# The end of layer 0: fills in runs of eight rows, the last chunk placed in two halves, counts one step earlier

## The reference

```python
x = x + ffn0(cond0(x))            # silu(x W1) * (x W3), Hadamard transform, W2
h = x W^T + scaled adapter(x)     # layer 1, condition: one of 8 adapters of rank 16 per batch
logits = h gate                   # 32 experts
w, idx = top_k(softmax(logits), 4); w = w / w.sum()
x = x + sum over the 4 chosen experts e of w_e * down_e(up_e(h) * silu(gate_e(h)))
```

## Time and profile before

| | |
|---|---|
| runs of the kernel | 1116.61 us median of 3, 1112.86 to 1117.81 |
| the profiled execution | 1120.59 us, of which its span is 1118.8 us |
| PE busy / weight loads | 898.6 us (80%) / 693.5 us |
| DVE, ACT, POOL busy | 565.7, 357.8 and 354.0 us |
| mean granted clock of PE | 0.894 |
| layer 0's last product ends / first block load is issued | about 214.8 us / 272.2 us |

### The profile page before, as it was taken

How to read it: one execution, slowest core, us unless ns; L and a number is a source line. 1 busy time by engine, 2 the same in 40 slices (tenths; PEclk the granted TensorE clock), 3 DMA queues, 4 the chain that set the end, 5 groups by cost and what they waited for, 6 DMA issues and landing times.

```text
span 1118.8 us, 17568 instructions
## 1 busy us (share of the span) xinstructions
PE 898.6 (80%) x5301; PEld 693.5 (62%) x5301; DVE 565.7 (51%) x1656; ACT 357.8 (32%) x996; POOL 354.0 (32%) x387
## 2 busy tenths in 40 slices
PE   2999898701999999698338768897996898999976
PEld 2778676501777777574236656787644676777765
DVE  5646775420565655158427666855252434444322
ACT  3434242320333333011126655750252222221210
POOL 7100616271455555113433434200046102333000
PEclk9999898965999999898658988996996998999997
DMA  9051206465544443482257778600052202332131
GB/s 346 12 188 38 77 4 241 154 223 169 182 128 132 126 131 87 156 276 79 77 118 172 167 157 174 157 36 1 27 167 86 86 5 67 107 99 72 53 104 46
DMA packets 71900, 132.25 MB, mean 118 GB/s; under 512 B 19652, under 2 KB 54237, under 8 KB 69347
## 3 DMA queue, kind: packets, MB, share of 16 engines
q1 hardware_dynamic: 49027, 75.81, 22.4%
q0 software_dynamic: 20480, 53.19, 17.7%
q10 hardware_dynamic: 2304, 2.13, 0.6%
HBM read 87.39 MB, written 43.30 MB: 117 GB/s over the span
## 4 chain that ended last, share of the span: by engine, by line
PE 29%; DMA 10%; issue 5%; DVE 3%; ACT 2%; SPq 1%; another core or an unknown queue 1%; POOL 1%; DVEq 0%; POOLq 0%; ACTq 0%
PE ps L442 8%; PE ps L680 4%; PE ps L698 3%; DMA early<-early 3%; DMA early<-newblk,new_i 2%; PE ps L2295 2%; DMA big<-early 2%; PE ps L2147 1%; PE ps L2189 1%; PE ps L2250 1%; DMA big<-newblk,new_i 1%; DMA early<-big 1%; SPq L920 1%; PE ps L2116 1%; DMA early<-in_cache,win_i 1%
## 5 line engine op out<-in xcount | busy, mean ns | idle before, releaser
L764 POOL DMA_INDIRECT sent_d<-mid,slot_i x88 | 94.8, 1078 | 134.3 <-DVE mid L598 88.7
L755 POOL DMA_INDIRECT back_d<-early,mid x95 | 93.8, 987 | 103.7 <-DVE early L739 70.5
L698 PE MATMUL ps<-early 96*128 (+1 forms) x346 | 100.0, 389 | 0.3 <-DVE early L733 0.2
L726 DVE TENSOR_TENSOR early<-early,ps 128x96 f32<-128x96 f32 (+1 forms) x134 | 37.3, 278 | 116.6 <-ACT early L714 77.9
L680 PE MATMUL ps<-big,early 128*128 x380 | 89.5, 360 | 5.9 <-ACT early L709 3.4
L709 ACT ACTIVATE early<-ps 128x256 f32<-128x256 f32 x134 | 51.3, 383 | 133.4 <-PE ps L670 122.9
L476 DVE TENSOR_TENSOR hidl<-work,hidh 128x512 fp32r<-128x512 f32 (+1 forms) x56 | 38.7, 691 | 102.6 <-ACT hidh L469 97.0
L670 PE MATMUL ps<-late,mid 128*128 128x128 f32 x268 | 53.6, 283 | 34.8 <-DMA mid<-sent_d 34.8
L482 ACT ACTIVATE work<-ps 128x512 f32<-128x512 f32 (+1 forms) x56 | 33.3, 595 | 149.2 <-PE ps L442 134.9
L755 POOL DMA_INDIRECT back_d<-big,mid x39 | 38.4, 984 | 118.5 <-DVE big L739 114.3
L680 PEld LDWEIGHTS ps<-big,early 128*128 128x128 f32 x380 | 62.6, 198 | 19.3 <-issue 16.4
(11 more groups left out here) (384 smaller groups left out, 2105.5 us busy)
## 6 DMA issues: line engine op xcount, KB each, us to landing
mid<-sent_d SPq DMA_DIRECT2D x134, 130.0 KB
big<-back_d SPq DMA_DIRECT2D x16, 512.0 KB
early<-back_d SPq DMA_DIRECT2D x16, 256.0 KB, 3.3
sent_d<-big SPq DMA_DIRECT2D x26, 130.0 KB
early<-in_w SPq DMA_DIRECT2D x3, 1024.0 KB, 11.7
big<-in_gate SPq DMA_DIRECT2D x1, 3072.0 KB, 12.2
big<-in_up SPq DMA_DIRECT2D x1, 3072.0 KB, 19.5
early<-in_gu SPq DMA_DIRECT2D x1, 2816.0 KB, 10.9
```

The costliest lines, as they stand in the source:

```text
L698: last = nc.tensor.matmul(ps[:, 6 + j % 2, 0:D], L.hTb[j % 2][0:f1 - f0, h * P:(h + 1) * P], L.down[0:f1 - f0, h, bass.ds(owners[j] * D, D ...
L726: nc.vector.tensor_tensor(L.hb[j % 2], L.sgb[j % 2], ps[:, 2 + j % 2, F:2 * F], ALU.mult)\
L755: nc.gpsimd.indirect_dma_start(out=back_d, out_offset=bass.IndirectOffsetOnAxis(ap=xblk[b % XRING][:, D:D + 1].bitcast(I32), axis=0), in_= ...
L764: nc.gpsimd.indirect_dma_start(out=sent_d, out_offset=bass.IndirectOffsetOnAxis(ap=L.slot_i[:, i:i + 1], axis=0), in_=L.rows[c][:, t, n, : ...
```

## The change

- Fills of layer 1: a fill still writes the same 128 rows of `sent_d`, but from 16 partitions that hold eight rows each (`FILL` = 8, `fill_rows`), so as 16 pieces of 8,320 B. `filler` is now 2,080 words of `work` on each partition, written by DVE in two memsets and a third for the mark, where GpSimd wrote it before. The partitions rotate with the expert's number. Layer 3 keeps its fills (`filler3`).
- The last chunk is two pieces of two tiles (`pieces`). Each is chosen, counted, numbered and weighted by itself; GpSimd's first half of scatters needs only the first. `dve_ends` and the table follow the second half's share products.
- In the steps: `pe_count` moves from m=6 to m=5, `act_share` in front of step 6's silu, `dve_slots` in front of step 6's product, and the share with its products from the end of m=7 to the end of m=6.
- SP issues the second weight load (`l1_up`) only when the scatters of chunks 0 and 1 have landed.
- ACT calls Exp and Silu once each on one column (`warm`) ahead of the last chunk's routing and behind it.

```diff
+        filler = work[:, 0:FILL * ROWW]
...
+L1.pieces = [(c, 0, TPC) for c in range(NCH - 1)] + [(NCH - 1, 0, 2), (NCH - 1, 2, TPC)]
+L3.pieces = [(c, 0, TPC) for c in range(NCH)]
...
+        def dve_slots(dve, ch, L, n):
+
+            c, t0, t1 = L.pieces[n]
+            tiles, w, bank = slice(t0, t1), (t1 - t0) * L.E, L.count_banks[n]
+            shape = [P, t1 - t0, L.E]
+            dve.wait_ge(s["counted_ps"], L.n0 + n + 1)
+            if n >= 1:
+                dve.wait_ge(s["slots_ready"], L.n0 + n)
...
+        def fill_rows(r, e):
+            p0 = (e * (P // FILL)) % P
+            return sent_d[bass.ds(r, P), :].rearrange("(q r) n -> q (r n)", r=FILL), filler[p0:p0 + P // FILL, :]
...
             sp.dma_start(l1_gate, a["gate1"]).then_inc(s["big1"], 16)
+            sp.wait_ge(s["sent_late"], 2 * HALF_SENT)
             sp.dma_start(l1_up, a["up1"]).then_inc(s["big1"], 16)
...
-                sp.dma_start(sent_d[bass.ds(r, P), :], filler).then_inc(s["filled"], 16)
+                sp.dma_start(*fill_rows(r, e)).then_inc(s["filled"], 16)
...
-                if c == NCH - 2:
-                    pool.wait_ge(s["index"], AT_TOKST)
-                    nc.gpsimd.memset(filler[:, 0:D], 0.0)
-                    nc.gpsimd.memset(filler[:, D:ROWW].bitcast(I32), int(FAR)).then_inc(s["fill_set"], 1)
...
-                    pool.wait_ge(s["numbered"], c + 1)
+                    pool.wait_ge(s["numbered"], c + 1 + (h if c == NCH - 1 else 0))
...
+                    if tc >= 1 and m == 6:
+                        act_share(act, L1, tc - 1)
                     if m < M0:
                         act_silu(act, m, P, tc * M0)
-                    if tc >= 1 and m == 6:
-                        act_share(act, L1, tc - 1)
...
+            nc.scalar.activation(warm[:, 0:1], C["ones"][:, 0:1], ACT.Exp)
             for t in range(TPC):
                 act_logits(act, NCH - 1, t)
+            act_share(act, L1, NCH - 1)
             for t in (0, 1):
                 act_copies(act, NCH - 1, t)
-            act_share(act, L1, NCH - 1)
+            act_share(act, L1, NCH)
             for t in (2, 3):
                 act_copies(act, NCH - 1, t)
 
+            nc.scalar.activation(warm[:, 1:2], C["ones"][:, 0:1], ACT.Silu)
...
+                    if tc >= 1 and m == 6:
+                        dve_slots(dve, ch, L1, tc - 1)
                     dve.wait_ge(s["silu_ready"], tc * M0 + (m + 1))
...
                     if tc >= 1 and m == 6:
-                        dve_slots(dve, ch, L1, tc - 1)
-                    if tc >= 1 and m == 7:
                         dve.wait_ge(s["poolhigh"], 1)
                         dve_share(dve, ch, L1, tc - 1)
...
             dve_residual(dve, NCH - 1, 0)
+            ch.link(nc.vector.memset(filler[:, 0:FILL * ROWW // 2], 0.0))
             dve_adapter(dve, NCH - 1)
-            for t in range(TPC):
+            ch.link(nc.vector.memset(filler[:, FILL * ROWW // 2:FILL * ROWW], 0.0))
+            nc.vector.memset(filler.rearrange("p (r n) -> p r n", n=ROWW)[:, :, D:ROWW].bitcast(I32), int(FAR))\
+                .then_inc(s["fill_set"], 1)
+            for t in (0, 1):
                 dve_best(dve, ch, L1, NCH - 1, t)
             dve_chosen(dve, ch, L1, NCH - 1)
+            for t in (2, 3):
+                dve_best(dve, ch, L1, NCH - 1, t)
             dve_slots(dve, ch, L1, NCH - 1)
             dve_share(dve, ch, L1, NCH - 1)
             dve_share_half(dve, NCH - 1, 0)
+            dve_chosen(dve, ch, L1, NCH)
+            dve_slots(dve, ch, L1, NCH)
+            dve_share(dve, ch, L1, NCH)
+            dve_share_half(dve, NCH - 1, 1)
             dve_ends(dve, ch, L1)
             dve_table(dve, L1, 6)
-            dve_share_half(dve, NCH - 1, 1)
...
-                    if tc >= 1 and m == 6:
+                    if tc >= 1 and m == 5:
                         pe.wait_ge(s["rows_sb"], (tc - 1) * TPC + 3)
                         pe_count(pe, L1, tc - 1)
...
             pe_count(pe, L1, NCH - 1)
+            pe_count(pe, L1, NCH)
```

More of the change, by code:

```diff
@@ L67 @@
 O_CREDIT = 16
+FILL = 8
 MAGIC = 1.5 * 2 ** 23
@@ L139, with __init__ @@
 class Experts:
-    def __init__(self, experts, chosen, shared, width, parts, total, blocks, tile0, chunk0, block0, turn0, table0):
+    def __init__(self, experts, chosen, shared, width, parts, total, blocks, tile0, piece0, block0, turn0, table0):
         self.E, self.K, self.F, self.parts, self.NB = experts, chosen, width, parts, blocks
@@ L392, in build @@
         kcol = sb("kcol", [P, 2, TPC * 12])
+        warm = sb("warm", [P, 4])
         wrows = mid[:, 2048:2560].rearrange("p (i n) -> p i n", i=NT)
@@ L521, in pe_rows, with pe_count @@
                 .then_inc(s["rows_ps"], 1)
-        def pe_count(pe, L, c):
-            pe.wait_ge(s["chosen_ready"], L.c0 + c + 1)
-            n, E, chosen, bank = TPC * L.E, L.E, L.chosen, L.count_banks[c]
-            for t in range(TPC):
[L528 to L532, removed]
+        def pe_count(pe, L, n):
+            c, t0, t1 = L.pieces[n]
+            pe.wait_ge(s["chosen_ready"], L.n0 + n + 1)
+            E, tiles, bank = L.E, t1 - t0, L.count_banks[n]
+            w = tiles * E
+            chosen = L.chosen[:, t0:t1, :]
+            for t in range(tiles):
+                nc.tensor.matmul(ps[:, bank, w:w + E], onesb, chosen[:, t, :], start=(t == 0), stop=(t == tiles - 1))
+            nc.tensor.matmul(ps[:, bank, 0:w], earlier, chosen, start=True, stop=False)
+            for t in range(tiles - 1):
+                later = tiles - 1 - t
+                last = nc.tensor.matmul(ps[:, bank, (t + 1) * E:w], onesb,
                                         chosen[:, t:t + 1, :].broadcast_to([P, later, E]),
-                                        start=False, stop=(t == TPC - 2))
+                                        start=False, stop=(t == tiles - 2))
             last.then_inc(s["counted_ps"], 1)
@@ L600, in dve_share_half, with dve_chosen @@
                 .then_inc(s["share_sb"], 1)
[L602 to L608, removed]
+        def dve_chosen(dve, ch, L, n):
+            c, t0, t1 = L.pieces[n]
+            dve.wait_ge(s["found_best"], L.i0 + c * TPC + t1)
+            tiles = slice(t0, t1)
+            shape = [P, t1 - t0, L.K, L.E]
+            top = L.best[:, c * TPC + t0:c * TPC + t1, :]
+            nc.vector.tensor_tensor(L.share[:, c * TPC + t0:c * TPC + t1, :], top[:, :, 0:L.K],
+                                    top[:, :, 0:1].broadcast_to([P, t1 - t0, L.K]), ALU.subtract)\
```

77 lines of the change are left out of this document (40 added, 37 removed).

## The result

The changed kernel took 1108.0 us (median of 13 runs, 1101.9 to 1112.1) against 1120.9 us for the kernel before on the same chip (13 runs, 1111.9 to 1128.4). The ratio is 0.9887, 95% interval 0.986 to 0.9913: 1.1% faster, some 12.7 us. The forecast was 1092 us and a gain of 24.9 us. Some runs fall into a slower state (9 of the 31 of the kernel before that stand beside z1 to z4, and 3 of z1's 10), and all ratios compare fast runs alone. The profiled execution has a span of 1106.2 us, 12.6 less than before.

The account below looks back on a forecast made before the run. PE's wait for the first block load, held by fills and then scatters, was taken as the bound. Load at 247.3 instead of 272.20 gains 24.9 us: 1120.6 − 24.9 = 1095.7 profiled, 1092 as a median; range 1084 to 1108.

Parts of the forecast that it names:

- What bounds it, and the lever: Between layer 0 and layer 1's experts: PE waits 34.3 us for the first block load; fills end last, before them scatters.
- Steps moved: Layer 0, share and counts one step up: chunk 2's scatters start at 202.3, 12.2 us before 214.46.
- rival 4: More than forecast: PE's clock holds its upper level through chunks 2 and 3, up to 5 us more, 1087; chance 0.05.
- rival 1: Fills stay slow beside scatters, one per 3.9 us: first load 259.8, gain 12.4, 1104 us; chance 0.22.
- The count: Counts moved one step up on PE: `chosen` is ready for chunk 1 with 0.6 us to spare.
- Up weights: Second weight load behind the scatters: costs nothing; ACT's 8.47 us and PE's 2.80 us waits are gone either way.
- Last chunk in halves: Wins the 1.14 us hand-over pause; placing stays hidden despite two late answers of 2.8 us; scatters end at 244.4.
- Added wait: Second half's share product, ahead of the ends, waits for chunk 2's late scatters; fills start at 227.5, today 237.44.
- Fills in runs of eight: Layer 1's fills as 16 descriptors instead of 128: 1.07 us each, 16 fills ending at 244.6.
- rival 3: Few source partitions: 16 serve a fill more slowly, 1.28 us each; first load 250.6, gain 21.6, 1095; chance 0.05.
- The base of the sum: Profiled execution 1120.59 us, taken as 4.0 above the median of 1116.61; the gain was subtracted from there.
- After the load: Everything behind the first block load at 272 hangs on the blocks and moves with them.

Follow-up runs that it names:

- z1: Changed kernel with the old 128-descriptor fills and with counts and share products back at their old steps; 0.9973 of the kernel before.
- z4: Changed kernel with fills from every seventh partition, started only when all scatters have landed; 1.0011 of the kernel before.
- z2: Changed kernel with the old 128-descriptor fills and without the wait holding back the up weights; 0.9882 of the kernel before.
- z3: Changed kernel with the old 128-descriptor fills and the expert ends ahead of the second share product; 0.9892 of the kernel before.
- x4: Changed kernel with the old fills of 128 descriptors from 128 partitions, faster kind of chip; 0.9882 of the kernel before.
- y2: The changed kernel without any edit, on the faster kind of chip; 0.9960 of the kernel before.
- v3: Changed kernel with old fills, last chunk in one piece, second share product behind ends and table; 0.9878 of the kernel before.
- y3: Changed kernel with the down weights loaded only when both halves of the last chunk are numbered; 0.9974 of the kernel before.
- x3: Changed kernel, eight-row fills from 16 neighbouring partitions, started only when all scatters have landed; 1.0069 of the kernel before.
- v4: Changed kernel with the old 128-descriptor fills, started only when all scatters have landed; 1.0032 of the kernel before.
- y1: The kernel before itself, without any edit, run again on the faster kind of chip; 0.9996 of the kernel before.
- v2: Changed kernel with the old 128-descriptor fills, a repeat of x4; 0.9876 of the kernel before.
- x1: Changed kernel with each fill's 16 source partitions every seventh instead of neighbours; 0.9887 of the kernel before.

## Why the prediction was right and where it failed

**What bounds it, and the lever: right.** The joint between layer 0 and the blocks was the place, and the fills ended last, now as before: 259.4, against 246.4 for the scatters.

**Steps moved: right, a little better than forecast.** Chunk 2's first scatter came 15.0 us earlier; I had 12.2. PE's longest wait for `work` fell from 3.3 to 1.5 us, that for xT only from 3.8 to 3.4. All low stretches of the clock before 217 us are gone in this profile, and the forecast had counted on one of them (1.7 us). That is the condition of rival 4 (0.05), which came true beside rival 1; z2, z3, x4, y2 and v3 keep one low stretch of 3.4 us near 167 us and start chunk 2's scatters as early, so the clock alone does not decide that start. The count fitted for chunk 1 and cost 2.2 us of waiting for chunk 2 instead of 2.80. v3, with the moved steps and the later up weights and little else, has a ratio of 0.9878. On one chip z2 has 0.9882 and z1, without the moved steps, 0.9973: they carry the gain.

**Up weights: right.** z2 shows the wait to be worth nothing beside the moved steps. I had said that ACT's 8.47 us wait would be gone; it fell to 3.73, and PE's from 2.80 to 2.2.

**Last chunk in halves: the size failed.** The forecast was 1.14 us won and a hidden placing, with two late answers of 2.8 us. ACT idled 5.84 and 5.46 us for them, so the halves were placed and weighted by 225.0 and 228.7 and the string paused 5.58 us. The kernel before and z1 to z4, on the same kind of chip, show such idle times too (up to 3.4 us in before and z1, up to 6.9 in z4), and no run of the other kind does: there ACT sits idle 1.26 us ahead of each of these logits. What makes them stays open: DVE, ACT and PE are free, and y3, which moved the down weights that are loading just then, ran on a kind of chip without the lag.

**Added wait: right in mechanism.** It held the ends on the faster kind for 4.33 us. On the chip of the result the late logits hid it. Fills from 230.06 instead of 227.5: 2.6 us of the miss.

**Fills in runs of eight: this is the step that failed.** "I take 1.07, because what slows it today appears only where many small descriptors of both kinds meet, and a fill then brings an eighth of them." It was 1.83, and 16 times 0.76 is 12.2 us of the 15.2 us by which the load was late; 0.5 more came between the last fill and the load. Of the 12.2, the 7 fills beside the scatters make 11.2 (2.67 instead of 1.07) and the 9 after them 1.0 (1.18). Two things were wrong in it. What slows a fill beside the scatters does not go away with fewer descriptors: z2, with 128 of them to a fill, has the same 2.67, and the register moves reach 0.70 us in both. This is rival 1, with 0.22, which gave 259.8 and 1104 us, nearest to the result; its price of 3.9 per fill was too high for either shape, since it was that of the slowest stretch. And the price without scatters was taken from a row of another shape: from 16 neighbouring partitions a fill costs 1.30 us (x3), not 1.10 (v4). This is rival 3, with 0.05, whose 1.28 per fill was right but was applied alone. What makes SP's instructions slow in that overlap stays open. The edit that I had costed at −2.8 us per fill beside the scatters costs about 6.5 us at the load on the faster kind of chip and shows no gain on the slower one (262.5 against z2's 260.2).

**The base of the sum.** The forecast of 1092 started from 1116.61, the median of 3 runs, and took the profiled 1120.59 as 4.0 above the usual. The median of 13 runs is 1120.9. So of the 16 us between 1092 and 1108.0, 4.3 are the base and 12.2 the gain that did not come.

**After the load.** The load came 9.7 us earlier and the span is 12.6 shorter; the other 2.9 are within what executions of one kernel differ by (1101.9 to 1112.1), and no run here assigns them.

## What to carry to other kernels

Before changing the shape of a string of transfers, look for the row that prices the new shape, and if there is none, count how many source partitions a transfer reads, not only its descriptors: fewer, longer descriptors from neighbouring partitions made the DMA engines busier for the same bytes. Where instructions that move no data take much longer than their median, as the register moves did here, the cause may be absent on another chip (y1) and gone when the overlap is (z4). So before a change is aimed at it, the same transfers should be tried with the overlap taken away. And a pace should be taken over the whole stretch that the change is to replace, not over its slowest part. What remained of the gain came from starting the strings earlier, and that held on both kinds of chip (0.9876 to 0.9892).

## What the runs showed of the hardware

- The same kernel takes 1119 to 1121 us on two of the five chips and 1070 to 1072 on three. Of the 49 us between the spans of before and y1, 11.4 stand at the first block load and the rest behind it. On the slower kind, register moves of SP and ACT take up to 0.71 us while fills and GpSimd's scatters overlap (median 0.03), and ACT takes the last chunk's last logits 2.3 to 8.8 us after PE's record of them, where y1, y2 and v2 have 0.04. Neither appears on the other kind, where no move of a fill takes over 42 ns. In z4 the overlap was taken away on the slower kind, and the slow moves were gone from the fills; they come back from 280 us on, in the blocks.
- A source of every seventh partition makes the issue of a 16-descriptor transfer take 0.529 us instead of 0.315, and its packets about half as long (0.37 instead of 0.69 us on ACT's queue). The longer issue is there on both kinds of chip (0.528 in x1, 0.529 in z4).
- The register load of a list's end, 0.27 us in v4 and 0.28 in z4 (DMA shares 0.68 and 0.53), takes 0.48 us in x3 and 0.49 in v2, where the shares are 0.87 and, from 226 to 240 us, 0.90 (medians). That the one makes the other is not shown.
- The DMA share alone misleads: 0.87 in x3 goes with long packets from 16 neighbouring partitions at 189 GB/s, while v4 moves 234 GB/s at a share of 0.68.
